# One core of a transformer block with gated attention and a mixture of experts: one norm chain for both norms, the x rows ahead of Wv and Wo, W2 split on GpSimd, the router bias inside the router weights

## The chip, the cores and the metric

One NeuronCore of one Trainium2 chip runs the whole program. The metric is the device time of one execution in microseconds (us). A core has TensorE (PE), VectorE (DVE), ScalarE (ACT), GpSimd (POOL) and SyncE (SP), which here only issues DMAs. Every engine takes its own instructions strictly in order and waits on semaphores.

## The reference

128 batches of 64 rows of 128 features are normed, attend to a context with 16 heads and a mask that is added, and are added back; the sum is normed again and goes through eight experts, of which each row uses its best two.

```python
def xattn(q, k, v, attn_mask, Wq, Wk, Wv, Wo, num_heads):
    qh, kh, vh = proj_heads(q, Wq), proj_heads(k, Wk), proj_heads(v, Wv)
    scores = einsum('bhqd,bhkd->bhqk', qh, kh) + attn_mask
    probs = softmax(scores, axis=-1)
    ctx = einsum('bhqk,bhkd->bhqd', probs, vh)
    return einsum('bse,de->bsd', ctx.transpose(0, 2, 1, 3).reshape(b, s, -1), Wo)

def ffn(x, Wg, bg, W1, b1, W2, b2):
    logits = xf @ Wg + bg
    w, idx = top_k(softmax(logits), 2)
    w = w / sum(w)
    comb = sum(one_hot(idx, 8) * w[..., None], axis=1)
    h = relu(einsum('nd,edh->enh', xf, W1) + b1[:, None, :])
    y = einsum('enh,ehd->end', h, W2) + b2[:, None, :]
    return einsum('end,ne->nd', y, comb)

x = x + tanh(g_xattn[0]) * xattn(layernorm(x), ctx, ctx, mask, Wq, Wk, Wv, Wo, 16)
x = x + tanh(g_ffn[0]) * ffn(layernorm(x), Wg, bg, W1, b1, W2, b2)
```

## The kernel before

**Numbers in two halves.** Every float32 operand of a product is held as a float16 high part and a float16 low part (names end in H and L), and each product is three matmuls (`three_passes`, lines 49 to 52): high by high, low by high, high by low. So each result in a PSUM bank is read twice: ACT writes the high part from the bank, and DVE, or POOL by way of a float32 copy in SBUF, writes the low part as the difference. Weights are scaled by WS = 32 before they are split.

**Groups and steps.** A group is eight batches (512 rows); there are 16 groups. Each engine has one loop over steps s, eight to a group (`for s in range(FIRST, LAST)`), and inside a step it works on several stages at once: the queries of the next group (two heads a step), values and scores of batch s, the softmax of batch s-1, the transposed probabilities of batch s-2, probabilities times values of batch s-3, and expert s-16 of the group two before. Step i of a group has the extra work: in step 4 the statistics of the second norm and both norm chains on POOL, in step 5 the normed rows on ACT, in step 6 the transposes of x, the context and x2 on PE, in step 0 the router logits, in steps 1 to 4 the ranks, the two gate weights and the bias b2. The order in each engine's loop is written by hand. For the first group the loop begins at s = -8.

**PSUM.** Two banks belong to the scores. The other six go round in turn (`take_bank`, `evicted`): a stage that takes a bank waits until the readers of whatever held it six turns earlier are done. PE therefore waits for DVE, ACT and POOL both through operands and through banks.

**The opening.** Ahead of the loop PE multiplies Wq by Wk (line 392, four banks), transposes Wv and Wo (line 403), then the normed rows of the first group (line 282). ACT norms these rows (line 527) before it takes the first weight bank. DVE takes the low halves of all weights, those of Wg and b2 included (line 661), and only then the low half of the transposed rows (line 686), which the first query waits for. SP loads Wq, Wk, x, Wv, Wo, Wg, b2 in this order, then the rest. W1 gets the bias b1 added and is split by ACT and DVE in steps 6 and 10, W2 in steps 11 and 12 (`SPLIT_W`).

**The norm chain** (`ln_scale_shift`, POOL, lines 896 to 905) is four instructions for each norm and group: variance plus EPS, power -1/2, minus the mean, shift. In step 4 it runs twice in a row, for the first norm of group g+2 and the second of group g-1. Behind it on POOL stands the low part of the hidden values (line 920), which the expert's second product waits for.

**The logits** (DVE, line 851): the bank is scaled and the bias `bgrow` added into SBUF tensor `logit`; `above` and `same` (lines 859, 860) compare each with each, then maximum and difference to it (861, 863). All four read `logit` in SBUF. The bank is free after line 851.

## Time and profile before

| | |
|---|---|
| median of 3 runs | 1015.77 us (1014.31 to 1018.8) |
| the profiled execution | 1016.24 us, of which the span of its instructions is 1014.5 us |
| PE busy | 976.2 us |
| DVE, ACT, POOL busy | 858.9, 865.7, 786.5 us |
| PE clock granted, mean over the span | 0.998 of full |
| DMA | 56.92 MB, mean 56 GB/s |

Busy time is the union of an engine's instructions; what PE is not busy it waited, and the profile names the releaser. A wait for several semaphores is put down to the one that came last.

### The profile page before, as it was taken

Reading aid. Unit: us, or ns where it says so; the run is one execution under the profiler, and the core shown is the slowest. Engines: PE = TensorE matmul, PEld = TensorE weight load, DVE = VectorE, ACT = ScalarE, POOL = GpSimd, SP = SyncE. Lnnn points to the kernel's source line nnn. Section 1 sums busy time; section 2 is a strip of 40 time slices with the busy share of each in tenths; the row PEclk is TensorE's granted clock in tenths of the full one; section 3 lists DMA queues with packets and bytes.
Section 4 is the critical chain, followed back from the end, with each engine's and each line's share of the span. In section 5 each row is a group of like instructions: output and inputs, shape, how many; then the busy total and the mean of one; then the engine's idle time right before and its main releaser. Section 6 shows DMA issues by size and latency. Waiting matters only on the chain.

```text
span 1014.5 us, 36079 instructions
## 1 busy us (share of the span) xinstructions
PE 976.2 (96%) x13762; PEld 733.5 (72%) x13762; DVE 858.9 (85%) x1754; ACT 865.7 (85%) x1740; POOL 786.5 (78%) x799
## 2 busy tenths in 40 slices
PE   6899799999999999999999999999999999999897
PEld 4467577777777777777777777777777777778775
DVE  3899998988979889798888979898897988879687
ACT  3799889898998989989898998989899898989743
POOL 4155578788888878888887888878888887889955
PEclk9999999999999999999999999999999999999999
DMA  9334332232232233322323233233223322323100
GB/s 209 65 62 76 58 60 43 55 64 54 47 61 57 49 57 53 65 45 49 59 54 60 49 65 54 43 57 62 53 51 58 59 38 44 54 34 61 26 13 22
DMA packets 319978, 56.92 MB, mean 56 GB/s; under 512 B 288920, under 2 KB 319680, under 8 KB 319808
## 3 DMA queue, kind: packets, MB, share of 16 engines
q1 hardware_dynamic: 319808, 54.61, 29.8%
q8 instruction: 112, 1.84, 0.8%
q14 instruction: 58, 0.48, 0.2%
HBM read 16.82 MB, written 4.19 MB: 21 GB/s over the span
## 4 chain that ended last, share of the span: by engine, by line
PE 67%; POOL 13%; DVE 7%; ACT 6%; issue 6%; DMA 1%; POOLq 0%; SPq 0%; DVEq 0%; ACTq 0%
PE bank L50 20%; PE bank L52 20%; PE bank L51 20%; PE bank L327 4%; POOL hidL L920 4%; POOL rstd L901 3%; POOL ptL L970 2%; PE bank L282 2%; DVE above L859 2%; POOL prob L976 1%; DVE y_scaled L747 1%; ACT pt L596 1%; ACT bank L539 1%; ACT vH L576 1%; ACT qH L488 1%
## 5 line engine op out<-in xcount | busy, mean ns | idle before, releaser
L920 POOL TENSOR_TENSOR hidL<-hid,hidH 128x512 f16<-128x512 f32 x228 | 261.1, 1162 | 0.0
L970 POOL TENSOR_TENSOR ptL<-pt,ptH 128x512 f16<-128x512 f32 x128 | 148.5, 1160 | 126.9 <-ACT pt L596 126.8
L681 DVE TENSOR_TENSOR qL<-bank,qH 128x512 f16<-128x512 f32 x248 | 169.4, 686 | 42.5 <-ACT qH L488 37.1
L488 ACT ACTIVATE qH<-bank 128x512 f16<-128x512 f32 x256 | 153.7, 603 | 46.0 <-PE bank L52 44.1
L50 PE MATMUL bank<-w2H,hidH 128*128 128x128 f16 x1024 | 178.1, 219 | 6.1 <-POOL hidL L920 5.7
L965 POOL TENSOR_TENSOR x<-x,y_scaled 128x512 f32<-128x512 f32 x128 | 163.4, 1277 | 21.1 <-DVE x L765 15.7
L52 PE MATMUL bank<-w2H,hidL 128*128 128x128 f16 x1024 | 178.1, 219 | 0.0
L51 PE MATMUL bank<-w2L,hidH 128*128 128x128 f16 x1024 | 178.1, 219 | 0.0
L514 ACT ACTIVATE hidH<-bank 128x512 f16<-128x512 f32 x256 | 166.5, 652 | 12.7 <-PE bank L52 12.0
L505 ACT ACTIVATE hid<-bank 128x512 f32<-128x512 f32 x228 | 146.8, 644 | 0.0
L976 POOL TENSOR_TENSOR prob<-prob,row_inv 128x512 f32<-128x512 f32 x128 | 133.7, 1045 | 2.7 <-DVE row_inv L793 1.9
L747 DVE SCALAR_TENSOR_TENSOR y_scaled<-bank,out_scale,weight 128x512 f32<-128x512 f32 x128 | 95.1, 743 | 42.5 <-PE bank L52 39.9
L50 PEld LDWEIGHTS bank<-w2H,hidH 128*128 128x128 f16 x1024 | 100.1, 98 | 17.5 <-issue 9.9
L51 PEld LDWEIGHTS bank<-w2L,hidH 128*128 128x128 f16 x1024 | 100.1, 98 | 7.6
L50 PE MATMUL bank<-xtH,aH 128*128 128x512 f16 x256 | 98.2, 383 | 6.4 <-DVE qL L681 3.1
L50 PEld LDWEIGHTS bank<-ctH,qH 128*128 128x128 f16 x1024 | 92.3, 98 | 15.2 <-issue 0.2
L50 PE MATMUL bank<-ptH,vdH 128*128 128x64 f16 x1024 | 103.0, 193 | 0.2 <-issue 0.2
L52 PE MATMUL bank<-ctH,qL 128*128 128x64 f16 x1024 | 103.1, 193 | 0.0
L52 PE MATMUL bank<-ptH,vdL 128*128 128x64 f16 x1024 | 103.1, 193 | 0.0
L51 PE MATMUL bank<-ctL,qH 128*128 128x64 f16 x1024 | 103.1, 193 | 0.0
L51 PE MATMUL bank<-ptL,vdH 128*128 128x64 f16 x1024 | 103.1, 193 | 0.0
L50 PE MATMUL bank<-ctH,qH 128*128 128x64 f16 x1024 | 103.0, 193 | 0.0
(145 smaller groups left out, 3444.8 us busy)
## 6 DMA issues: line engine op xcount, KB each, us to landing
vdH<-vH SPq DMA_DIRECT2D x256, 64.0 KB, 2.3
vdL<-vL SPq DMA_DIRECT2D x256, 64.0 KB, 2.3
x_raw<-in_x SPq DMA_DIRECT2D x16, 256.0 KB, 3.1
ctx_raw<-in_ctx SPq DMA_DIRECT2D x16, 256.0 KB, 3.2
mask_raw<-in_fside_Bx1xSxS SPq DMA_DIRECT2D x32, 128.0 KB, 2.9
out_x<-x SPq DMA_DIRECT2D x16, 256.0 KB, 2.6
qH<-in_L_xattn_Wq SPq DMA_DIRECT2D x2, 256.0 KB, 4.9
qH<-in_L_xattn_Wk SPq DMA_DIRECT2D x2, 256.0 KB, 5.6
```

Source lines behind the costliest of these rows:

```text
L50: e.matmul(dst, lhs[0], rhs[0], start=start, stop=False, skip_group_check=True)
L51: e.matmul(dst, lhs[0], rhs[1], start=False, stop=False, skip_group_check=True)
L52: return e.matmul(dst, lhs[1], rhs[0], start=False, stop=stop, skip_group_check=True)
L488: act.activation(qH[:, g % 2, 2 * j + g2, :, h2, :], bk("Q", g, h)[:, :].rearrange("p (b q) -> p b q", b=GB), ACT.Copy).then_inc(s_q_high, 1)
L505: act.activation(hid[:, k % NR, :], bk("hid", g, e, c)[:, :], ACT.Relu).then_inc(s_relu[c], 1)
L514: act.activation(hidH[:, m % 2, c, :], bk("hid", g, e, c)[:, :], ACT.Relu).then_inc(s_hid_high[c], 1)
L681: dve.tensor_tensor(qL[at], bk("Q", g, h)[:, :].rearrange("p (b q) -> p b q", b=GB), qH[at], ALU.subtract).then_inc(s_q_low[h % 2], 1)
L747: dve.scalar_tensor_tensor(y_scaled[:, m % 2], bk("y", yg, yi)[:, :].rearrange("p (t d) -> p t d", t=GT), out_scale[:, 1:2], weight3[:, :, ...
L920: pool.tensor_tensor(hidL[:, m % 2, c, :], hid[:, k % NR, :], hidH[:, m % 2, c, :], ALU.subtract).then_inc(s_hid_low[c], 1)
L965: pool.tensor_tensor(acc, acc, y_scaled[:, m % 2], ALU.add).then_inc(s_y_add, 1)
L970: pool.tensor_tensor(ptL[:, b % 2, :], pt[:, b % 2, :], ptH[:, b % 2, :], ALU.subtract).then_inc(s_pt_low, 1)
L976: pool.tensor_tensor(p, p, row_inv[:, b % NPB, :].unsqueeze(2).to_broadcast([P, JG, S]), ALU.mult).then_inc(s_normal, 1)
```

## The change

Five edits, in the order of the program.

1. **Loads and opening order.** SP loads x after the first halves of Wq and Wk, ahead of their second halves. PE transposes the normed rows ahead of Wv and Wo; ACT takes two weight banks before it norms the rows, and its high half of the transposed rows, like DVE's low half, moves ahead of Wv and Wo.
2. **Wg and b2** have their own SBUF tensors, and their halves are taken in step 3 and not in the opening.
3. **The router bias**: bg/8 minus the first row of Wg is added to all rows of Wg in step 0 (a small DVE instruction more); the logit bank then holds logits with bias, scaled by 32. DVE copies the bank to `logit`, and the comparisons read one operand from the copy and one from the bank, the maximum and the difference the bank alone; the bank is free only after these. The exponent takes the scale.
4. **W2** is split by POOL in steps -4 and -2, three instructions of 128x1024 for each half, and no longer by ACT and DVE in steps 11 and 12.
5. **The norm chain** (`norm_scale_shift`) runs once per group for both norms, on 128x8 where there were two of 128x4, in the order variance, minus the mean, power, shift.

```diff
+NORM_LAG = 3
-SPLIT_W = (6, 10, 11, 12)
+SPLIT_W1 = (6, 10)
+SPLIT_W2 = (-4, -2)
...
+        wg_in = sb("wg_in", [P, E])
+        b2_in = sb("b2_in", [STACK, D])
...
+            if kind == "logit":
+                return [(s_gt, at[0] + 1), (s_eq, at[0] + 1), (s_gshift, at[0] + 1)]
...
 @block.tensor
             pe.wait_ge(s_ident, 1)
+            transposes("xT", 0, xhat, (s_ln[0]["rows"], 1), s_xT)
             for k, (what, raw) in enumerate((("Wv", wv_raw), ("Wo", wo_raw))):
...
-            transposes("xT", 0, xhat, (s_ln[0]["rows"], 1), s_xT)
...
 @block.scalar
-                    act.wait_ge(s_wdve, H // 4 + 6)
+                    act.wait_ge(s_wpe, H // 4 + 4)
...
             def ln_rows(w, g, src, dst, freed):
-                act.wait_ge(s_ln[w]["shift"], g + 1)
+                act.wait_ge(s_norm_shift, g + 1 + (NORM_LAG if w else 0))
...
-            ln_rows(0, 0, x_raw[:, 0], xhat[:, :, :], None)
             for n in range(H // 4):
+                if n == 2:
+                    ln_rows(0, 0, x_raw[:, 0], xhat[:, :, :], None)
...
+            transposed_high("xT", 0, xtH[:, 0, :], s_xT, None, s_xT_high)
...
+                if s == 3:
+                    act.wait_ge(s_wg_lifted, 1)
+                    act.activation(wgH[:, :], wg_raw, ACT.Copy, scale=WS).then_inc(s_wact, 1)
+                    act.wait_ge(s_load["b2"], 16 * 3)
+                    act.activation(b2_halves[:, :], b2_raw, ACT.Copy, scale=WS).then_inc(s_wact, 1)
...
-                if s in SPLIT_W[2:]:
-                    n = SPLIT_W.index(s) - 2
-                    act.wait_ge(s_load["W2" + "ab"[n]], 16)
-                    act.activation(flat_w2[0][:, n * 1024:(n + 1) * 1024], w2_raw[n], ACT.Copy, scale=WS).then_inc(s_wact, 1)
...
 @block.vector
+            transposed_low("xT", 0, xtL[:, 0, :], xtH[:, 0, :], s_xT_high, s_xT_low)
...
-            weights_low(H // 4 + 4, wgL[:, :], wg_raw, wgH[:, :])
-            weights_low(H // 4 + 5, b2_halves[QUAD:QUAD + E, :], b2_raw[QUAD:QUAD + E], b2_halves[QUAD:QUAD + E, :])
-            transposed_low("xT", 0, xtL[:, 0, :], xtH[:, 0, :], s_xT_high, s_xT_low)
...
+                    dve.tensor_tensor(wg_raw, wg_raw, bgrow[:, :], ALU.add).then_inc(s_wg_lifted, 1)
+                if s == 3:
+                    weights_low(H // 4 + 4, wgL[:, :], wg_raw, wgH[:, :])
+                    weights_low(H // 4 + 5, b2_halves[QUAD:QUAD + E, :], b2_raw[QUAD:QUAD + E], b2_halves[QUAD:QUAD + E, :])
...
-                    l, m, e_ = logit[:, g % 2], logit_max[:, g % 2], expo[:, g % 2]
+                    l = bk("logit", g - 2)[:, 0:GT * E].rearrange("p (t e) -> p t e", t=GT)
+                    m, e_ = logit_max[:, g % 2], expo[:, g % 2]
...
-                    dve.scalar_tensor_tensor(l, bk("logit", g - 2)[:, 0:GT * E].rearrange("p (t e) -> p t e", t=GT),
-                                             1.0 / WS, bgrow[:, :].unsqueeze(1).to_broadcast([P, GT, E]), ALU.mult,
-                                             ALU.add).then_inc(s_logit_in, 1)
-                    lj = l.unsqueeze(2).to_broadcast([P, GT, E, E])
+                    dve.tensor_copy(logit[:, g % 2], l).then_inc(s_logit_in, 1)
+                    lj = logit[:, g % 2].unsqueeze(2).to_broadcast([P, GT, E, E])
                     li = l.unsqueeze(3).to_broadcast([P, GT, E, E])
...
 @block.gpsimd
+            def norm_scale_shift(k):
+                both = slice(0 if k < GROUPS else 1, 2 if k >= NORM_LAG else 1)
+                for w, n in ((0, k), (1, k - NORM_LAG)):
+                    if within(n, GROUPS):
+                        pool.wait_ge(s_ln[w]["aggr"], n + 1)
+                        if n:
+                            pool.wait_ge(s_ln[w]["rows"], n)
+                pool.tensor_scalar(rstd[:, both], meanvar[:, both, :, 1], EPS, None, ALU.add).then_inc(s_norm_var, 1)
+                pool.tensor_scalar(minus_mean[:, both], meanvar[:, both, :, 0], -1.0, None, ALU.mult).then_inc(s_norm_minus, 1)
+                pool.wait_ge(s_norm_var, k + 1)
+                pool.tensor_tensor(rstd[:, both], rstd[:, both], minus_half[:, both], ALU.pow).then_inc(s_norm_rstd, 1)
+                pool.wait_ge(s_norm_rstd, k + 1)
+                pool.wait_ge(s_norm_minus, k + 1)
+                pool.tensor_tensor(shift[:, both], minus_mean[:, both], rstd[:, both], ALU.mult).then_inc(s_norm_shift, 1)
...
+                if s in SPLIT_W2:
+                    n = SPLIT_W2.index(s)
+                    half = slice(n * 1024, (n + 1) * 1024)
+                    pool.wait_ge(s_load["W2" + "ab"[n]], 16)
+                    pool.tensor_scalar(flat_w2[0][:, half], w2_raw[n], WS, None, ALU.mult).then_inc(s_w2_high, 1)
+                    pool.tensor_scalar(w2_raw[n], w2_raw[n], WS, None, ALU.mult).then_inc(s_w2_scaled, 1)
+                    pool.wait_ge(s_w2_high, n + 1)
+                    pool.wait_ge(s_w2_scaled, n + 1)
+                    pool.tensor_tensor(flat_w2[1][:, half], w2_raw[n], flat_w2[0][:, half], ALU.subtract).then_inc(s_w2, 1)
...
-                if within(g + 2, GROUPS) and i == 4 - sooner:
-                    ln_scale_shift(0, g + 2)
-                if within(g - 1, GROUPS) and i == 4:
-                    ln_scale_shift(1, g - 1)
+                if within(g + 2, GROUPS + NORM_LAG) and i == 4 - sooner:
+                    norm_scale_shift(g + 2)
```

How the instructions move on two engines. On DVE in the opening, before the change (aL, wvL and woL are low halves of weights, xtL that of the first rows, qL of the queries):

```order
L661 SCALAR_TENSOR_TENSOR aL<-bank,aH 128x512 [waits weights_high] x4
L705 SCALAR_TENSOR_TENSOR wvL<-bank,wvH 128x256 [waits weights_high]
L705 SCALAR_TENSOR_TENSOR wvL<-bank,wvH 128x256
L705 SCALAR_TENSOR_TENSOR wvL<-bank,wvH 128x256 [waits weights_high]
L705 SCALAR_TENSOR_TENSOR wvL<-bank,wvH 128x256
L661 SCALAR_TENSOR_TENSOR woL<-bank,woH 128x512 [waits weights_high] x2
L661 SCALAR_TENSOR_TENSOR wgL<-qL,wgH 128x8 [waits weights_high]
L661 SCALAR_TENSOR_TENSOR b_halves<-qL,b_halves 8x128 [waits weights_high]
L686 TENSOR_TENSOR xtL<-bank,xtH 128x512 [waits xT_high]
L681 TENSOR_TENSOR qL<-bank,qH 128x8x64 [waits q_high] x4
```

The same place with the change:

```order
L662 SCALAR_TENSOR_TENSOR aL<-bank,aH 128x512 [waits weights_high] x4
L687 TENSOR_TENSOR xtL<-bank,xtH 128x512 [waits xT_high]
L707 SCALAR_TENSOR_TENSOR wvL<-bank,wvH 128x256 [waits weights_high]
L707 SCALAR_TENSOR_TENSOR wvL<-bank,wvH 128x256
L707 SCALAR_TENSOR_TENSOR wvL<-bank,wvH 128x256 [waits weights_high]
L707 SCALAR_TENSOR_TENSOR wvL<-bank,wvH 128x256
L662 SCALAR_TENSOR_TENSOR woL<-bank,woH 128x512 [waits weights_high] x2
L682 TENSOR_TENSOR qL<-bank,qH 128x8x64 [waits q_high] x4
```

xtL stood behind twelve instructions on weights and now stands behind the four aL alone.

On POOL, from the last fill of the opening to the first low half of queries of group 1, before:

```order
L946 MEMSET vdL 128x4096
L899 TENSOR_SCALAR rstd<-meanvar 128x4 [waits ln0_aggr,minus_half]
L901 TENSOR_TENSOR rstd<-rstd,minus_half 128x4 [waits ln0_var]
L902 TENSOR_SCALAR minus_mean<-meanvar 128x4
L905 TENSOR_TENSOR shift<-minus_mean,rstd 128x4 [waits ln0_minus,rstd0]
L899 TENSOR_SCALAR rstd<-meanvar 128x4 [waits ln0_rows,ln0_aggr]
L901 TENSOR_TENSOR rstd<-rstd,minus_half 128x4 [waits ln0_var]
L902 TENSOR_SCALAR minus_mean<-meanvar 128x4
L905 TENSOR_TENSOR shift<-minus_mean,rstd 128x4 [waits ln0_minus,rstd0]
L913 TENSOR_TENSOR qL<-hid,qH 128x8x64 [waits q_out1,q_high]
```

With the change, from the second of these chains on:

```order
L900 TENSOR_SCALAR rstd<-meanvar 128x4 [waits ln0_rows,ln0_aggr]
L901 TENSOR_SCALAR minus_mean<-meanvar 128x4
L903 TENSOR_TENSOR rstd<-rstd,minus_half 128x4 [waits norm_var]
L906 TENSOR_TENSOR shift<-minus_mean,rstd 128x4 [waits norm_minus,norm_rstd]
L958 TENSOR_SCALAR w2H<-y_scaled 128x1024 [waits loaded_W2a]
L959 TENSOR_SCALAR y_scaled<-y_scaled 128x1024
L962 TENSOR_TENSOR w2L<-y_scaled,w2H 128x1024 [waits w2_scaled,w2_high]
L958 TENSOR_SCALAR w2H<-x 128x1024 [waits loaded_W2b]
L959 TENSOR_SCALAR x<-x 128x1024
L962 TENSOR_TENSOR w2L<-x,w2H 128x1024 [waits w2_scaled,w2_high]
L914 TENSOR_TENSOR qL<-hid,qH 128x8x64 [waits q_out1,q_high]
```

Six instructions of 128x1024 now stand between that chain and the queries' low half (w2_raw lies in the tensors y_scaled and x2 until they are needed), and minus_mean has moved ahead of the power.

## Rows read from the trace of the kernel before

**Rows 1.** Page, part 1: busy us of each engine (share of the span), instructions
```profile
PE 976.2 (96%) x13762; PEld 733.5 (72%) x13762; DVE 858.9 (85%) x1754; ACT 865.7 (85%) x1740; POOL 786.5 (78%) x799
```

**Rows 2.** Waits of PE, 160 to 900 us: releaser, us, times, longest
```profile
PE bank L50 <- POOL hidL L920: 5.0, 12, 0.4
PE bank L50 <- DVE y_scaled L747: 2.1, 12, 0.2
```

**Rows 3.** Waits of PE, 900 to 1000 us
```profile
PE bank L50 <- DVE y_scaled L747: 0.8, 2, 0.5
PE bank L50 <- POOL hidL L920: 0.7, 1, 0.7
```

**Rows 4.** Waits of PE, 95 to 125 us
```profile
PE bank L327 <- POOL prob L976: 4.6, 3, 2.9
```

**Rows 5.** Timeline of the opening: start us, us, instruction, count, [idle before, releaser]
```profile
6.52 7.16 PE L392 MATMUL bank<-qH 64*128 64x128 f32 x32 [4.12 <-DMA qH<-in_L_xattn_Wk]
...
7.27 3.50 POOL L946 MEMSET vdL<- 128x4096 f16 x1
...
11.66 0.23 POOL L899 TENSOR_SCALAR rstd<-meanvar 128x4 f32<-128x4 f32 x1 [0.89 <-DVE meanvar L674]
...
13.72 1.65 ACT L527 ACTIVATE xhat<-x_raw,shift,rstd 128x128 f32<-128x128 f32 x4 [11.65 <-POOL shift L905]
...
16.13 2.22 SPq L1029 DMA_DIRECT2D x<-in_L_ffn_W  x1
...
16.73 1.94 PE L403 MATMUL bank<-ident,qL 128*128 128x128 f32 x8 [1.15 <-DVE aL L661]
...
18.46 1.06 PE L282 MATMUL bank<-ident,xhat 128*128 128x128 f32 x4
...
22.11 0.58 PE L50 MATMUL bank<-xtH,aH 128*128 128x512 f16 x1 [2.58 <-DVE b_halves L661]
```

**Rows 6.** Timeline of PE and of POOL after the opening, 32 to 47 us
```profile
35.01 0.44 PE L50 MATMUL bank<-xtH,aH 128*128 128x512 f16 x1 [2.50 <-DVE qL L681]
...
46.64 1.16 POOL L913 TENSOR_TENSOR qL<-hid,qH 128x512 f16<-128x512 f32 x1 [14.66 <-ACT hid L496]
```

**Rows 7.** Timeline of DVE, steps 11 and 12: the low halves of W2
```profile
98.92 1.90 DVE L661 SCALAR_TENSOR_TENSOR w2L<-y_scaled,w2H 128x1024 f16<-128x1024 f32 x1
...
106.08 1.22 DVE L661 SCALAR_TENSOR_TENSOR w2L<-x,w2H 128x1024 f16<-128x1024 f32 x1
```

**Rows 8.** Timeline of POOL in step 4 of one group: two norm chains
```profile
460.76 0.23 POOL L899 TENSOR_SCALAR rstd<-meanvar 128x4 f32<-128x4 f32 x1
461.07 1.04 POOL L901 TENSOR_TENSOR rstd<-rstd,minus_half 128x4 f32<-128x4 f32 x1
...
462.87 0.23 POOL L899 TENSOR_SCALAR rstd<-meanvar 128x4 f32<-128x4 f32 x1
```

**Rows 9.** Timeline of DVE and of PE around that step
```profile
460.04 0.38 DVE L674 BATCH_NORM_AGGREGATE meanvar<-stats 128x2 f32<-128x6 f32 x4
...
466.14 0.22 PE L50 MATMUL bank<-w2H,hidH 128*128 128x128 f16 x1 [0.42 <-POOL hidL L920]
```

**Rows 10.** Timeline of DVE, POOL and PE in step 0 of a group: the logits
```profile
490.19 1.14 DVE L859 TENSOR_TENSOR above<-logit 128x256 f32<-128x256 f32 x1
491.25 0.41 DVE L860 TENSOR_TENSOR same<-logit 128x256 f32<-128x256 f32 x1
...
491.79 0.73 DVE L863 TENSOR_TENSOR expo<-logit,logit_max 128x32 f32<-128x32 f32 x1
492.44 0.74 DVE L747 SCALAR_TENSOR_TENSOR y_scaled<-bank,out_scale,weight 128x512 f32<-128x512 f32 x1
...
491.74 0.73 POOL L991 TENSOR_TENSOR same<-same,tri 128x256 f32<-128x256 f32 x1 [0.69 <-DVE same L860]
...
493.24 0.39 PE L50 MATMUL bank<-x2tH,w1H 128*128 128x512 f16 x1 [0.18 <-DVE y_scaled L747]
```

**Rows 11.** One stretch, busy us: PE, PEld, DVE, ACT, POOL, PEclk, DMA share, GB/s
```profile
36.00:42.00 6.00, 6.00 (x45) 3.17 (x44) 5.63 (x10) 5.13 (x11) 0.00 (x0) 0.78 0.00 0
```

71 lines of the change are left out of this document (26 added, 45 removed).

## The prediction

> **What bounds the kernel now.** I read the page first, then the waits of PE by stretch, then the timeline of each place that the change touches. PE is busy 976.2 of 1014.5 us [rows 1], so 38.3 us of waiting is all that an edit can win which leaves the matmuls alone, and this one does. The reader should see where that idle time lies. In each regular group PE waits 0.4 us once for the hidden values' low part on POOL and 0.2 us once for y_scaled on DVE: 5.0 + 2.1 = 7.1 us in the twelve groups from 160 to 900 us [rows 2]; two more groups bring 0.8 + 0.7 = 1.5 us [rows 3]. In steps 11 to 13, while the weights of the experts are still being split, PE waits 4.6 us for POOL's probabilities, once for 2.9 us [rows 4]. In the opening it waits 2.58 us ahead of the first query [rows 5], and 2.50 us more nine queries later [rows 6].
>
> **Opening.** Before, POOL waited 0.89 us for the statistics of x and began its chain at 11.66; ACT began the normed rows 2.06 us later, at 13.72, and only after them the first weight bank [rows 5]. With x loaded third, the statistics come before POOL has finished its fills, so that POOL begins at 11.66 - 0.89 = 10.77 (the 3.50 us fill that starts at 7.27 ends there). The chain loses the 0.24 us instruction between power and shift, which now runs beside the wait for the variance: 1.8 us. ACT starts the rows at 12.6, having taken two banks already, and is done 1.65 us later, at 14.25. PE ends Wq by Wk at 6.52 + 7.16 = 13.68, waits 0.6, transposes the rows (1.06 us), then Wv and Wo in two sets of eight at 1.94 us each: 14.3 + 1.0 + 3.9 = 19.2. DVE's low half of the rows falls under those transposes, so the first query starts at 19.2 and not 22.11: **2.9 us**. Both ends: with POOL as late as before, still the rows' transposes no longer stand behind two sets of transposes, and the low part of b2, which the first query waited for [rows 5], is gone: 1.5 us; a first query that already finds PE's clock up gives 4.2. Loading x ahead of the second halves of Wq and Wk puts these back by one load, and PE takes its second eight pairs only halfway through the 7.16 us; I cost that at nothing, at most 0.3 us.
>
> **The second chain** of POOL (the rows of group 1) is what DVE and ACT then stand behind until PE resumes at 35.01 [rows 6]. It loses the same 0.24 us: **0.25 us**.
>
> **W2 on POOL.** Six instructions of 128x1024 move to where POOL idled 14.66 us, up to 46.64 [rows 6]. No row has this shape. From below, the fill of 4096 elements in 3.50 us [rows 5] gives 0.9 us for 1024; from above, twice the 1.16 us of a two-operand 128x512 [rows 6] gives 2.3. So 5.4 to 14 us; I take 8, nearer the fill for the four with one operand. The room is 14.7 us, and both ends fit: **0**. SP issues the last W2 load by 16.13 + 2.22 = 18.35 [rows 5], ten microseconds ahead of POOL's turn. Rule and row here pull apart only in the size: the Trainium skill (GPSIMD Engine Reference, section 4.1, Engine selection) says elementwise work belongs on VectorE and is about twice as slow on GpSimd. By that rule alone the six cost twice what DVE paid, and the move would be wrong if POOL had a queue behind it; here the queue is empty.
>
> What the move takes away: DVE's 1.90 + 1.22 = 3.1 us of W2 low parts [rows 7], and ACT's two high halves, in the stretch where DVE has no idle time and PE waits 4.6 us for what DVE feeds to POOL [rows 4]. I take 3.0 for these. In step 12 the two chains become one, which frees POOL earlier for the probabilities, but ACT's first four rows now wait for the statistics of both norms; I put the balance at 0.7. Together **3.7 us**; ends 2.0 (PE catches another releaser) and 5.9 (4.6 and the smaller waits beside it, all gone).
>
> **What is put into step 0 and step 3.** A small addition in step 0 and the halves of Wg and b2 in step 3 are three small instructions more on DVE and two on ACT, of some 0.2 us each going by the 0.23 of POOL's [rows 8], where DVE is nearly full. PE is idle there only now and then, so I charge **-0.4 us**, ends 0 and -0.8.
>
> **The joined chain in the regular groups.** POOL starts the first chain at 460.76, the second at 462.87: 2.11 us for each [rows 8]. Both sets of statistics are there by 460.42 [rows 9], so the joined one need not wait. Its price turns on the power: 1.04 us on four elements a partition [rows 8], against 0.23 for the addition of the same shape ahead of it [rows 8]. If that is fixed, the joined chain takes 1.9 us; if it is per element, eight cost 2.0 and the chain 2.9. Either way the hidden values' low part comes 1.3 to 2.3 us earlier, and PE's wait for it is 0.42 [rows 9]. It goes entirely.
>
> **The logits.** DVE's `above` takes 1.14 us and `same`, with the same operands' shape, 0.41; the difference of 32 elements takes 0.73 and ends as POOL's `same` does (491.74 + 0.73 = 492.47) [rows 10]. An instruction with two SBUF operands thus stands still while POOL works. With one operand in PSUM they do not compete: 0.41 and about 0.2, **1.2 us** earlier for y_scaled, which PE waits 0.18 for [rows 10]. That wait goes too. The Trainium skill (SBUF — State Buffer, SBUF: two separate sides) calls the pair of ports shared by VectorE and GpSimd an exclusive lock, held for a whole instruction; by that rule, the trace agrees. The bank is held about a microsecond longer, but the stage that takes it next is the one behind PE's instruction at 493.24 [rows 10], 2 us after DVE will be done with it.
>
> Regular groups and the two late ones: **7.1 + 1.5 = 8.6 us**.
>
> **Sum.** 2.9 + 0.25 + 3.7 - 0.4 + 8.6 = 15.05 us. The profiled execution took 1016.24 us, 0.47 above the median of the runs: 1001.2, or 1000.7 against the median. I say 1001.0. The worst and the best ends added give 1016 - (1.5 + 0 + 2.0 - 0.8 + 7.1) = 1006.4 and 1016 - (4.2 + 0.5 + 5.9 + 8.6) = 997.
>
> **Rivals.**
> - *The regular groups give nothing back.* Once PE waits no longer for POOL or y_scaled, another wait appears at the same places; against it, PE's idle time there has two releasers only [rows 2]. Then only the gains of the opening and steps 11 to 13 remain, 6.45 us: 1009.8. It is near the bound between faster and the same.
> - *PE's clock.* After the wait of 2.50 us [rows 6] the granted clock from 36 to 42 us is 0.78 [rows 11], which is 2.6 us at the 1.2 GHz level and the rest at 2.4. If the shorter waits keep it at the upper level, half of the 2.6 falls away, and as much again at the first queries: 998.5. Against it: PE was busy for 7.16 us at a stretch in the opening, and still the query at 22.11 ran at the lower level (0.58 us [rows 5] where the same shape takes 0.39 [rows 10]). The Trainium skill (TensorE: Matmul & The Clock Gate, Part 1: The HAM clock gate) says that the clock is released by sustained activity, which the longer run of transposes ahead of the queries would now be.
> - *POOL overruns.* If its six W2 instructions cost over 2.5 us each, POOL is late for the queries' low part at 46.64 and then for the first probabilities; at 4 us each 24 us stand against a room of 14.6, the excess of 9.4 goes straight to PE, and 5.65 us of gain are left: 1010.6.
> - *Slower: compares against PSUM.* `above` and `same` read a bank with each element repeated eight times. No row has this. The slack that the change makes ahead of y_scaled is 1.0 us a group, after the 1.2 that it saves. If each comparison takes 1.7 us and not 0.41, DVE is 2.6 us later, PE waits 1.55 us in each of 15 groups, 23.3 us, while the other gains are 15.05 - 2.9 = 12.1: 1027. It outweighs them from about 1.3 us a comparison. For it: nothing. Against it: DVE reads 512 elements of a bank for y_scaled in 0.74 us [rows 10], so 256 should be about 0.4.
> - *It doesn't do what it says*: the joined chain or the moved loads could leave the order as it was; the order of instructions shows that they don't, and I give this nothing.
>
> **Chances.** Forecast 0.78; regular groups give nothing 0.09; clock 0.06; POOL overruns 0.03; slower by the comparisons 0.04. A measurement of this kernel can tell about 0.5%, 5 us, from no change: faster is below 1010.7. The forecast, the clock and most of the first rival lie there, 0.90; within 0.5% I put the rest of that rival and the overrun, 0.06; slower 0.04. The range 996 to 1008.5 takes in these ends, widened for the parts of the first rival, and the clock, and leaves out the other rivals.
>
> **What would show it.** The first query at 19 to 20 us; POOL's six W2 instructions between 29 and 43; steps 11 and 12 without W2 on DVE and PE's waits for probabilities there under 2 us; one power of 128x8 per group, and no wait of PE on hidL or y_scaled from 160 to 900 us, with groups 0.6 us shorter; `above` at 0.4 to 0.5 us. Wrong would be groups as long as before, comparisons over a microsecond, or a first query after 21 us.

## The result, and the profile after

| | before | after |
|---|---|---|
| median, us (runs) | 1015.66 (4) | 997.71, 997.37 to 998.24 (4) |
| ratio to before | 1 | 0.9823, 95% interval 0.9807 to 0.9839 |
| profiled execution, us | 1016.24 | 997.37 |
| its span, us | 1014.5 | 995.6 |

The change makes the kernel 18 us faster. I had forecast 1001.0, 15 us, with a range of 996 to 1008.5. Busy time of the engines (the page, part 1; before in [rows 1]), and then the six largest of the twelve releasers that PE waits for in the changed kernel (waits of PE: releaser, us, times, longest):

```profile
PE 970.8 (98%) x13762; PEld 734.2 (74%) x13762; DVE 837.9 (84%) x1753; ACT 863.2 (87%) x1738; POOL 786.0 (79%) x753
```

```profile
PE bank L332 <- POOL prob L986: 6.8, 9, 2.2
PE bank L397 <- DMA qH<-in_L_xattn_Wk: 4.0, 1, 4.0
PE bank L52 <- DVE qL L682: 2.3, 1, 2.3
PE bank L52 <- DVE xtL L687: 1.6, 1, 1.6
PE bank L388 <- POOL ptH L924: 1.4, 1, 1.4
PE bank L332 <- DVE hidH L829: 0.9, 1, 0.9
```

From 160 to 900 us the view of the waits lists nothing at all where it had two releasers in twelve groups [rows 2]. Idle time is down by 38.3 - 24.8 = 13.5 us, but the span by 18.9. The difference is the main lesson of this case: the idle time that the profile shows on PE is less than what a wait costs (below).

To see where the gain arises I use a mark that both kernels have once a step: the start of DVE's row maximum of step s. How much earlier it comes than before, beside what the terms of the forecast add up to:

| from | to | gain in the traces | forecast |
|---|---|---|---|
| start | step 0 (42.94, now 37.72) | 5.22 | 2.9 + 0.25 |
| step 0 | step 4 (59.19, now 56.73) | -2.76 | -0.4 |
| step 4 | step 13 (110.44, now 104.55) | 3.43 | 3.0 |
| step 13 | step 16 (127.28, now 122.52) | -1.13 | 0.7 |
| step 16 | end of the span | 14.14 | 8.6 |
| | sum | 18.9 | 15.05 |

**Opening.** The timeline answers to [rows 5] (start us, us, instruction, count, [idle before, releaser]):

```profile
12.71 1.65 ACT L531 ACTIVATE xhat<-x_raw,shift,rstd 128x128 f32<-128x128 f32 x4 [1.92 <-POOL shift L906]
...
14.51 1.09 PE L287 MATMUL bank<-ident,xhat 128*128 128x128 f32 x4 [0.73 <-ACT xhat L531]
...
15.39 3.27 PE L409 MATMUL bank<-ident,qL 128*128 128x128 f32 x16
...
18.50 0.38 PE L52 MATMUL bank<-xtH,aH 128*128 128x512 f16 x1
```

The chain of loads, norm and rows is within 0.2 us of the forecast (12.6 for the rows, 14.3 for their transposes). But the sixteen transposes of Wv and Wo take 3.27 us and not 3.9, and the first query 0.38 and not 0.58: PE's clock is at its upper level when the queries begin. Not all of that is the clock's: in e7_spread (below), whose first query still runs at the lower level (0.63 us), the sixteen transposes take 3.62.

**W2 on POOL.** What followed in the opening is the part that I had put at nothing:

```profile
26.73 2.79 POOL L958 TENSOR_SCALAR w2H<-y_scaled 128x1024 f16<-128x1024 f32 x1
...
40.16 2.13 POOL L962 TENSOR_TENSOR w2L<-x,w2H 128x1024 f16<-128x1024 f32 x1
42.24 1.16 POOL L914 TENSOR_TENSOR qL<-hid,qH 128x512 f16<-128x512 f32 x1
43.35 1.05 POOL L986 TENSOR_TENSOR prob<-prob,row_inv 128x512 f32<-128x512 f32 x1
...
44.55 0.63 PE L332 MATMUL bank<-ident,prob 128*128 128x128 f32 x4 [1.42 <-POOL prob L986]
```

The six instructions take 15.5 us (two of them are shown; the others stand between them), and POOL goes from the last one straight into its first queries, with no idle time: it is late, and PE waits 1.42 us for the first probabilities. What PE then does, in stretches of 1 us (busy time of PE, its count, granted clock, DMA share, GB/s):

```profile
45.00:46.00 1.00, 1.00 (x6) 0.74 0.06 10
46.00:47.00 1.00, 1.00 (x4) 0.50 0.78 122
47.00:48.00 1.00, 1.00 (x4) 0.50 0.54 74
48.00:49.00 1.00, 1.00 (x15) 0.56 0.48 72
49.00:50.00 1.00, 1.00 (x29) 1.00 0.00 0
```

It works at the 1.2 GHz level from 45.5 to 48.9 us. Once its clock has come up, the kernel before has one such stretch, ahead of step 0 [rows 11]. The changed kernel has one here and one from 110.3 to 113.7; a third begins at 994, when PE is nearly done.

**Regular groups.** One joined chain, in the place of the two in [rows 8]:

```profile
450.61 0.25 POOL L900 TENSOR_SCALAR rstd<-meanvar 128x8 f32<-128x8 f32 x1
450.94 0.24 POOL L901 TENSOR_SCALAR minus_mean<-meanvar 128x8 f32<-128x8 f32 x1
451.15 1.67 POOL L903 TENSOR_TENSOR rstd<-rstd,minus_half 128x8 f32<-128x8 f32 x1
452.90 0.20 POOL L906 TENSOR_TENSOR shift<-minus_mean,rstd 128x8 f32<-128x8 f32 x1
453.06 1.15 POOL L921 TENSOR_TENSOR hidL<-hid,hidH 128x512 f16<-128x512 f32 x1
```

Two and a half us instead of 4.2; the power costs 1.04 us on four elements a partition and 1.67 on eight, between my two readings of it. And the logits, against [rows 10]:

```profile
479.46 0.42 DVE L857 TENSOR_TENSOR above<-logit,bank 128x256 f32<-128x256 f32 x1
479.80 0.41 DVE L858 TENSOR_TENSOR same<-logit,bank 128x256 f32<-128x256 f32 x1
...
480.35 0.19 DVE L861 TENSOR_TENSOR expo<-bank,logit_max 128x32 f32<-128x32 f32 x1
```

A group has become 0.93 us shorter, where I had said 0.6.

### The profile page after: what moved, and what is told of

It is laid out like the page before. It is cut to its first block, busy times and chain, and to the rows that moved or that the text cites. A ratio compares the mean times of both kernels' runs of the same rounds, so it can differ in the third digit from the quotient of the medians.

```text
span 995.6 us, 36034 instructions
## 1 busy us (share of the span) xinstructions
PE 970.8 (98%) x13762; PEld 734.2 (74%) x13762; DVE 837.9 (84%) x1753; ACT 863.2 (87%) x1738; POOL 786.0 (79%) x753
## 3 DMA queue, kind: packets, MB, share of 16 engines
q8 instruction: 112, 1.84, 0.8%
## 4 chain that ended last, share of the span: by engine, by line
PE 87%; POOL 6%; DVE 3%; issue 2%; ACT 1%; POOLq 0%; DVEq 0%; ACTq 0%
PE bank L52 26%; PE bank L54 26%; PE bank L53 26%; PE bank L332 6%; PE bank L287 2%; POOL hidL L921 1%; PE bank L468 1%; POOL prob L986 1%; POOL x L975 1%; POOL w2H L958 1%; POOL ptL L980 0%; DVE qL L682 0%; PE bank L477 0%; DVE otL L803 0%; POOL vdH L946 0%
## 5 line engine op out<-in xcount | busy, mean ns | idle before, releaser
L518 ACT ACTIVATE hidH<-bank 128x512 f16<-128x512 f32 x256 | 168.9, 661 | 13.2 <-PE bank L54 12.5
L509 ACT ACTIVATE hid<-bank 128x512 f32<-128x512 f32 x228 | 148.9, 653 | 0.0
L52 PEld LDWEIGHTS bank<-ctH,qH 128*128 128x128 f16 x1024 | 92.4, 98 | 15.3 <-issue 0.3
L52 PEld LDWEIGHTS bank<-ptH,vdH 128*128 128x128 f16 x1024 | 92.2, 98 | 14.3 <-issue 0.8
```

What stands on the lines that cost most here:

```text
L52: e.matmul(dst, lhs[0], rhs[0], start=start, stop=False, skip_group_check=True)
L509: act.activation(hid[:, k % NR, :], bk("hid", g, e, c)[:, :], ACT.Relu).then_inc(s_relu[c], 1)
L518: act.activation(hidH[:, m % 2, c, :], bk("hid", g, e, c)[:, :], ACT.Relu).then_inc(s_hid_high[c], 1)
```

## The experiments

The kernels ran in four sets (e1 to e4, e5 to e8, e9 and e10, e11 and e12), each with its own runs of the kernel before, whose median lay between 1015.96 and 1017.91 us. Kernels of one set are compared by their times, those of different sets by their ratios to the kernel before, or by their traces. The diffs are excerpts.

### One part alone, on the kernel before

**e1_join**, the joined chain:

```diff
-                if within(g + 2, GROUPS) and i == 4 - sooner:
-                    ln_scale_shift(0, g + 2)
-                if within(g - 1, GROUPS) and i == 4:
-                    ln_scale_shift(1, g - 1)
+                if within(g + 2, GROUPS + NORM_LAG) and i == 4 - sooner:
+                    norm_scale_shift(g + 2)
```

> Kernel before with the joined norm chain alone. Theory (the wait shown for PE, 0.42 us, is counted from the end of the last matmul, while the pitch of the matmuls is shorter, so that what is lost is 0.58 us): the joined chain ends the wait on hidL in the 12 regular groups and in two late ones, 14 x 0.58 = 8.1 us, and 0.25 us comes from the second chain in the opening; 1015.7 - 8.4 = 1007.3. A POOL instruction of 128x8 pow takes 1.67 us once a group, groups are 0.58 us shorter (59.57), and the wait on y_scaled stays at 0.18. Rival A (only what the waits show): 14 x 0.42 + 0.25 = 6.1, 1009.6, groups 0.42 shorter. Rival B (the two waits hide one behind the other, so that without the edit of the logits nothing is gained): 1015.5, groups as long as before, the wait on y_scaled grown to 0.6.

Measured 1009.89 (1008.87 to 1010.71), ratio 0.9930, 0.9913 to 0.9947. The time falls on rival A's price by chance: the groups are 0.58 us shorter, as the theory said. Most of what is missing is 0.9 us in the opening, where PE's clock comes up only at 27.7 us (at 25.0 in the kernel before), so that step 0 is 0.65 later and not 0.25 earlier, and 1.17 us between steps 13 and 14, the same as in the change (see e12_apart).

**e2_open**, the opening's order:

```diff
             pe.wait_ge(s_ident, 1)
+            transposes("xT", 0, xhat, (s_ln[0]["rows"], 1), s_xT)
...
-            transposes("xT", 0, xhat, (s_ln[0]["rows"], 1), s_xT)
```

> Kernel before with the new opening order alone (x loaded third, its transposes ahead of those of Wv and Wo). Theory (the 5.2 us won by the first row maximum of DVE are all the opening's; what is lost again by step 4 comes from W2 on POOL and from the small instructions of step 3): first row maximum at 37.9, and of the 5.0 us at least 4.5 are still there at step 4 and at the end; 1015.7 - 4.8 = 1010.9. Rival (steps 0 to 4 are bound by DVE whatever the opening does, so that the gain falls to 2.5 there): first row maximum at 37.9, the one of step 4 at 56.7, 1013.2.

Measured 1013.93 (1011.90 to 1013.99), ratio 0.9967, 0.9955 to 0.9979: 2 us, and not the 4.8 of the theory. Step 0 comes 3.48 us earlier, not 5.0, and steps 0 to 14 keep it, so that the rival is wrong too, though its 1013.2 is the nearer number. At step 15 1.63 us are lost, in a stretch at the lower clock from 112.2 to 115.6 us that the kernel before does not have (PE in stretches of 1 us):

```profile
113.00:114.00 1.00, 1.00 (x14) 0.50 0.00 0
114.00:115.00 1.00, 1.00 (x7) 0.50 0.12 20
```

**e3_w2pool**, W2 on POOL:

```diff
-SPLIT_W = (6, 10, 11, 12)
+SPLIT_W = (6, 10)
+SPLIT_W2 = (-4, -2)
```

> Kernel before with W2 split on POOL in steps -4 and -2 alone. POOL's six instructions take 15.5 us from 31.9 on, to 47.4; the queries' low part that POOL began at 46.64 before comes about 0.9 us late. Theory (off DVE and ACT in steps 11 and 12 they win 3.0, in the opening they lose 1 to 1.5 through POOL's lateness and the two-operand instructions of DVE that stand still beside them): 1015.7 - 1.7 = 1014.0, with the start of step 14 0.5 to 2 us earlier than before. Rival A (steps 11 to 13 are bound by the two separate norm chains of POOL there, and what W2 takes on DVE is hidden): no gain, only the loss, 1016.9. Rival B (the loss is larger, as all of what is lost between steps 0 and 4 is POOL's): 1015.2.

Measured 1015.75 (1013.71 to 1016.73), ratio 0.9991, 0.9980 to 1.0001: no gain that can be measured, where the theory had 1.7 us. The trace has both of its parts: 1.43 us lost from step 0 to 4, and 2.96 won from step 8 to 13.

**e11_logit**, Wg, b2 and the logits:

```diff
-                    dve.scalar_tensor_tensor(l, bk("logit", g - 2)[:, 0:GT * E].rearrange("p (t e) -> p t e", t=GT),
-                                             1.0 / WS, bgrow[:, :].unsqueeze(1).to_broadcast([P, GT, E]), ALU.mult,
-                                             ALU.add).then_inc(s_logit_in, 1)
-                    lj = l.unsqueeze(2).to_broadcast([P, GT, E, E])
+                    dve.tensor_copy(logit[:, g % 2], l).then_inc(s_logit_in, 1)
+                    lj = logit[:, g % 2].unsqueeze(2).to_broadcast([P, GT, E, E])
```

> Kernel before with the edits of Wg, b2 and the logits alone (bias inside the weights, their halves in step 3, comparisons with one operand in the bank); the two norm chains, the opening and W2 as before. Theory (the two waits of a group are independent, each lost time adds): above falls to 0.42, the wait on y_scaled goes (0.35 us lost in each of 14 groups, 1.4 in the first one), the wait on hidL stays at 0.42, groups of 59.80; the opening wins 1.7 (no low part of b2 ahead of the first query) and steps 3 and 4 lose up to 1.9 again: 1015.9 - 6.2 + 0.2 = 1009.9. Together with the joined chain alone (6.1) and the opening alone (2.0) this makes 14.1 of the 18. Rival (the parts hide each other, the y_scaled wait is only moved to hidL of the next expert): groups of 60.15, 1014 to 1015.

Measured 1010.87 (1010.02 to 1011.37), ratio 0.9928, 0.9916 to 0.9941; the groups are 59.80 us, as the theory said.

The four reductions are 0.70, 0.33, 0.09 and 0.72%, together 1.84%, where the whole change gives 1.77%. The medians of the sets give less, 6.1 + 2.0 + 0.2 + 7.0 = 15.3 of 18 us, and so do the spans of the profiled executions, 5.5 + 2.3 + 1.2 + 5.4 = 14.4 of 18.9. The gap does not arise in the regular groups: at step 32 the four together are 1.7 us ahead and the change 7.0. A good part of it is PE's clock, which comes up 1.0 to 2.7 us later in e1_join, e3_w2pool and e11_logit than in the kernel before, and costs e2_open 1.63 us at step 15. All the sums say which parts carry the change: the chain and the logits.

The mark of each step shows where each gains (us earlier than in the kernel before; negative is later):

| | step 0 | 4 | 13 | 14 | 16 | 17 | 32 | 112 |
|---|---|---|---|---|---|---|---|---|
| the change | 5.22 | 2.46 | 5.89 | 4.73 | 4.76 | 6.29 | 7.03 | 16.29 |
| e1_join | -0.65 | -0.64 | -0.63 | -1.80 | -1.79 | -1.80 | -0.62 | 5.17 |
| e2_open | 3.48 | 3.49 | 3.50 | 3.52 | 1.90 | 1.90 | 1.96 | 2.20 |
| e3_w2pool | -0.87 | -2.30 | 0.71 | 0.73 | 0.73 | 0.73 | 0.81 | 1.12 |
| e11_logit | -0.26 | -1.60 | -1.14 | -1.13 | -1.13 | 0.15 | -0.41 | 3.13 |

From step 32 to step 112 are ten groups. Their length follows from the marks: before (848.22 - 246.68) / 10 = 60.15 us, e1_join 59.58, e11_logit 59.80, the change 59.23. The joined chain takes 0.58 from each group, the logits 0.35, and the sum of 0.93 is what the change takes: two waits that add, and neither hides the other. In e1_join PE still waits for y_scaled, in e11_logit still for hidL, as in [rows 2] (waits of PE, 160 to 900 us, of the one and of the other):

```profile
PE bank L51 <- DVE y_scaled L748: 2.1, 12, 0.2
```

```profile
PE bank L50 <- POOL hidL L925: 5.0, 12, 0.4
```

**Why 0.58 and not 0.42.** The timeline of PE in the kernel before, around the wait of [rows 9]:

```profile
465.45 0.22 PE L51 MATMUL bank<-woL,otH 128*128 128x128 f16 x1
465.50 0.22 PE L52 MATMUL bank<-woH,otL 128*128 128x128 f16 x1
```

These matmuls of 128x128 start 0.056 us apart (465.45 and 465.50 are rounded), and each is shown with 0.22 us from start to end. The idle time of 0.42 is counted from the end of the last, 465.72, up to 466.14. But without the wait the next would have started at 465.50 + 0.056, so what is lost is 0.58. At y_scaled four transposes stand ahead, shown with 0.64 us, behind which the next instruction can start after 0.47 (in the changed kernel, 108.92 to 109.39): 493.24 - 492.42 - 0.47 = 0.35, where the profile has 0.18 [rows 10]. Both agree with the lengths of the groups to a hundredth. The forecast for e1_join had the 0.58 before it ran.

### Which half of the logits' edit matters

**e4_logit_sbuf**: the changed kernel, all four readers on the SBUF copy.

```diff
                     lj = logit[:, g % 2].unsqueeze(2).to_broadcast([P, GT, E, E])
+                    l = logit[:, g % 2]
                     li = l.unsqueeze(3).to_broadcast([P, GT, E, E])
```

> Changed kernel, but above, same, the maximum and the difference read both operands from the SBUF copy; the bias stays folded into the weights. Theory (an instruction of DVE with two SBUF operands stands still while POOL works): above takes 1.0 to 1.2 us again in most groups, the difference 0.5 to 0.7, y_scaled comes about 1 us later, PE waits for it and loses 0.35 us per group: 997.7 + 15 x 0.35 = 1002.9, groups of 59.58. Rival A (it was the folding of the bias that made them short, the operands' place doesn't matter): above stays at 0.42, 997.7. Rival B (above grows, but the joined chain has made enough room ahead of y_scaled): above at 1.1 and no wait of PE, 997.9.

Measured 1003.96 (1003.39 to 1004.16): 6.3 us slower than the changed kernel (by the ratios, 0.9871 against 0.9823, 4.9; the theory had 5.2). Groups are 59.57 us. The lines of DVE by shape (min, median and longest ns, first and last start) for e4, and below them for the change:

```profile
L858 DVE TENSOR_TENSOR above<-logit x16: 426/1132/2322, 124.8 to 975.4; 128x256 f32<-128x256 f32 x16
```

```profile
L857 DVE TENSOR_TENSOR above<-logit,bank x16: 420/420/422, 124.7 to 969.5; 128x256 f32<-128x256 f32 x16
```

The same instruction on the same shape takes 0.42 us with one operand in PSUM, and up to 2.3 with both in SBUF. The folding of the bias into the weights wins nothing by itself (its groups are as long as those of e1_join, 59.58); it is what allows the operand to stay in the bank. The timeline of e4 in one group shows DVE held until POOL is done, at 482.61, and `above` ending 0.28 us behind that; in the groups before it the distance is 0.28 or 0.29 us as well:

```profile
481.45 1.16 POOL L922 TENSOR_TENSOR hidL<-hid,hidH 128x512 f16<-128x512 f32 x1
481.76 1.13 DVE L858 TENSOR_TENSOR above<-logit 128x256 f32<-128x256 f32 x1
```

So an instruction of DVE with two SBUF operands stands still until an instruction of POOL with two operands is done. The Trainium skill (SBUF — State Buffer, SBUF: two separate sides) calls it an exclusive lock, held for the whole instruction; by that rule, the trace agrees here. It does not for POOL's multiplications by a constant (e7_spread, below).

### What the opening gave back

**e5_w2back**: the changed kernel, W2 split by ACT and DVE in steps 11 and 12 again.

```diff
+                if s in (11, 12):
+                    n = s - 11
+                    act.wait_ge(s_load["W2" + "ab"[n]], 16)
+                    act.activation(flat_w2[0][:, n * 1024:(n + 1) * 1024], w2_raw[n], ACT.Copy, scale=WS).then_inc(s_wact, 1)
```

> Changed kernel with W2 split by ACT and DVE in steps 11 and 12 again, as before; all other edits kept. Theory (W2 on POOL costs in the opening what it wins in steps 11 to 13: POOL is free only at 42.3, 0.9 us late for its first queries, PE waits 1.42 us for the probabilities and then runs 3.4 us at the 1.2 GHz level): the start of step 4 is 1.5 to 2.3 us earlier than in the changed kernel and has no stretch at half the clock ahead of it, the start of step 14 is about 0.7 later, and the whole is within 1.5 us of the changed kernel: 998.5. Rival (what I forecast: the move is worth 3 us and costs nothing): 1000.7, with step 4 where it is in the changed kernel.

**e6_small**: all that Wg and b2 need, in step -5.

```diff
-                if s == 0:
+                if s == -5:
                     dve.wait_ge(s_load["bg"], 16)
...
-                if s == 3:
+                if s == -5:
                     weights_low(H // 4 + 4, wgL[:, :], wg_raw, wgH[:, :])
```

> Changed kernel with the addition to Wg and the halves of Wg and b2 in step -5, where ACT waits for the shift and DVE has no work, and nothing of them in steps 0 and 3. Theory A (of the 2.76 us lost between steps 0 and 4 the instructions put into step 3 take the larger part, since step 3 to 4 alone loses 1.85): step 4 starts 1.5 to 1.9 us earlier than in the changed kernel, 996.0. Theory B (the loss is POOL's lateness and the stretch at half the clock that follows PE's wait): step 4 starts at most 0.6 us earlier, 997.2 to 997.7. A loss of some tenths is possible if ACT's part delays its rows: step 0 would then start later.

**e7_spread**: the second half of W2 behind the probabilities of steps 5, 6 and 7.

```diff
-SPLIT_W2 = (-4, -2)
+SPLIT_W2 = ((-4, -4, -4), (5, 6, 7))
```

> Changed kernel, but POOL takes only the first half of W2 in the opening (step -4), and the three instructions of the second half behind the probabilities of steps 5, 6 and 7, where it has gaps of 2.9 to 3.3 us. Theory B (POOL's lateness): POOL is free long before its first queries, PE's wait of 1.42 us for the probabilities falls to 0.6, no stretch at half the clock stands at 45 to 49 us, step 4 starts 0.9 to 2.8 us earlier, and it stays won: 996.0. Theory A (the small instructions of step 3): step 4 at most 0.5 us earlier, 997.3. If the gaps of POOL are too small for 2.8 us instructions, PE waits for ptL or the probabilities in steps 5 to 8 and the gain is given back: 998.

**e8_rows**: ACT's rows of group 1 one step later.

```diff
-                if i == 5 - sooner and within(g + 2, GROUPS):
+                if i == (4 if s < 0 else 5) and within(g + 2, GROUPS):
                     ln_rows(0, g + 2, x_raw[:, (g + 2) % NX], xhat[:, :, :], (s_xT, g + 2))
```

> Changed kernel with ACT's rows of group 1 one step later in the opening, so that ACT does not stand for 2.33 us at the shift of POOL while banks of queries wait. Theory (PE's wait of 2.29 us at 27.5 is ACT's wait for the shift and its 1.65 us of rows, put ahead of the queries): the wait falls to about 1 us and is followed by a smaller one for the rows; step 0 starts 1 to 1.7 us earlier, 996.4. Rival (the first wait only moves to the transposes of these rows, or PE's clock falls after the new pattern of waits): step 0 where it was or later, 997.7 to 999.

| | us | ratio, 95% interval | step 0 | 3 | 4 | 7 | 14 | 32 |
|---|---|---|---|---|---|---|---|---|
| e5_w2back | 999.47 | 0.9827, 0.9809 to 0.9844 | 0.05 | 0.90 | 1.46 | 1.46 | -1.51 | -1.97 |
| e6_small | 996.76 | 0.9799, 0.9782 to 0.9816 | -0.70 | 0.19 | 1.24 | 0.77 | 0.76 | 0.18 |
| e7_spread | 997.74 | 0.9807, 0.9789 to 0.9825 | -1.12 | -0.27 | 0.29 | -0.45 | -0.43 | -0.90 |
| e8_rows | 998.37 | 0.9819, 0.9797 to 0.9840 | 1.84 | 0.04 | 0.00 | -0.01 | -0.02 | -0.18 |

(The marks are here us earlier than in the changed kernel.) No interval excludes that one of the four is as fast as the change, and e7_spread (996.0 forecast) and e8_rows (996.4) missed their theories. The traces say more:

- Without W2 on POOL step 4 comes 1.46 us earlier, and no stretch at the lower clock stands there; in steps 11 and 12, 1.46 + 1.51 = 2.97 us are lost. So my 3.0 for ACT and DVE was right, and the nothing for POOL should have been 1.5.
- The 0.70 and 1.12 us that e6_small and e7_spread have lost by step 0 are not their edits'. They have them already at PE's first long wait, at 30.50 and 30.92 us against 29.80: PE's clock comes up 0.8 and 1.7 us after their first query. From step 0 to step 4 e6_small gains 1.94 us and e7_spread 1.41.
- The 2.76 us lost there have three parts. Us from mark to mark:

| | step 0 to 3 | 3 to 4 | lower clock between |
|---|---|---|---|
| before, e9_best | 10.89 | 5.36 | no |
| the change | 11.80 | 7.21 | yes |
| e3_w2pool | 11.79 | 5.89 | yes |
| e6_small | 10.91 | 6.16 | no |
| e5_w2back, e7_spread | 10.95 | 6.65 | no |

- Up to step 3, 0.9 us are lost only where the stretch at the lower clock is. e6_small has W2 on POOL as the change has, and PE's wait for it, but not the stretch (below: timeline of PE, and PE in stretches of 1 us). From step 3 to 4, POOL's lateness costs 0.6 to 0.8 us and the small instructions 1.0 to 1.3, of which 0.2 are lost to both. Theory A and theory B are both right, each for a part, and the 1.94 of e6_small holds the 0.9 of the clock.

```profile
45.26 0.41 PE L332 MATMUL bank<-ident,prob 128*128 128x128 f32 x2 [1.43 <-POOL prob L986]
```

```profile
47.00:48.00 1.00, 1.00 (x16) 1.00 0.70 104
```

- e8_rows wins 1.84 us at step 0 and has lost them at step 3. The place is one line (timeline of PE): POOL is where it was, so PE, who comes earlier, waits longer.

```profile
44.49 0.63 PE L332 MATMUL bank<-ident,prob 128*128 128x128 f32 x4 [3.21 <-POOL prob L986]
```

- e7_spread gave back 0.7 us at step 6. Timeline of POOL and DVE in it, and of DVE in the changed kernel: the low half of W1, which has two SBUF operands, now stands beside an instruction of POOL.

```profile
69.47 2.77 POOL L934 TENSOR_SCALAR x<-x 128x1024 f32<-128x1024 f32 x1
...
69.64 1.95 DVE L662 SCALAR_TENSOR_TENSOR w1L<-hidH,w1H 128x1024 f16<-128x1024 f32 x1 [0.63 <-ACT w1H L641]
```

```profile
69.92 1.23 DVE L662 SCALAR_TENSOR_TENSOR w1L<-hidH,w1H 128x1024 f16<-128x1024 f32 x1 [0.63 <-ACT w1H L641]
```

It grows by 0.72 us and ends at 71.59, before POOL's instruction, which ends at 72.24. In e6_small the low part of b2 likewise takes 1.06 us (0.28 in the kernel before, where POOL is idle) inside a multiplication of POOL of 2.79. So beside this one-operand form DVE is held for some 0.7 to 0.8 us and not for the whole instruction; why, these runs do not show.

**e9_best** joins the three, with W2's instructions placed clear of step 6 and the rows of e8.

```diff
+SPLIT_W2 = ((-4, -4, -4), (-2, 5, 7))
...
-                if s == 3:
+                if s == -4:
                     act.wait_ge(s_wg_lifted, 1)
...
-                if i == 5 - sooner and within(g + 2, GROUPS):
+                if i == (4 if s < 0 else 5) and within(g + 2, GROUPS):
```

> Changed kernel with three moves joined: ACT's rows of group 1 one step later in the opening (won 1.84 us at step 0 and lost them to POOL's lateness by step 3); W2 on POOL spread so that POOL is free when its first queries come: the first half and one instruction of the second in the opening, the other two in steps 5 and 7, which keep clear of the split of W1 in step 6, where a 128x1024 of DVE grew from 1.23 to 1.95 us beside POOL; Wg and b2 in steps -5 and -4, ahead of ACT's rows. Theory (the three losses are separate places of one chain): step 0 earlier by 1.0 to 1.8 than in the changed kernel, step 4 by 3.5 to 4.5, most of it kept; 994.0. Rival A (steps 5 to 13 are bound by DVE, whatever comes before gives at most what the single moves gave, 1.2): 996.5. Rival B (the new pattern of waits makes PE's clock fall elsewhere, 1.7 us each): 995.5.

Measured 993.31 (993.05 to 994.42), ratio 0.9777, 0.9762 to 0.9791: faster than the change. Step 0 comes 2.09 us earlier than in the changed kernel, step 4 4.85, and 4.4 are left at step 14. All of the 2.76 us between steps 0 and 4 are back, and the 1.84 that e8_rows had won at step 0 and lost now stay: the wait for POOL that ate them is gone. The other two moves were not stopped by one another; alone they show 1.24 and 0.29 us at step 4 because their profiles had lost 0.70 and 1.12 to the clock before step 0. e9_best has no stretch at the lower clock before 990 us.

### The clock, and step 12

**e10_fill**: the changed kernel with eight matmuls more, whose result is overwritten, in the wait ahead of the second stretch at the lower clock.

```diff
                 for freed in take_bank("PT", b):
                     pe.wait_ge(*freed)
+                for _ in range(8 if b in (11,) else 0):
+                    pe.matmul(bk("PT", b)[:, :], aH[:, 0, :], wvH[:, 0, :, :].rearrange("p c d -> p (c d)"),
+                              start=True, stop=True)
```

> Changed kernel with eight matmuls of 128x512 more, whose result is overwritten, in PE's wait of 2.15 us for the probabilities of step 13; they add no work that the reference asks for. Theory (the stretch at half the clock from 110.3 to 113.8 follows from that wait, and costs 1.2 us, the loss between steps 13 and 14): the granted clock stays at the upper level there, step 14 starts 1.0 to 1.3 us earlier, 996.6. Rival A (the stretch is there, but DVE or ACT sets step 14, so that PE's slow stretch costs nothing): clock up, step 14 where it was, 997.7. Rival B (it doesn't hang on this wait): clock still at half from 110 to 114, time unchanged.

Measured 997.57 (997.40 to 997.79), as the change. The clock is 1.00 from 109 to 114 us now, where the changed kernel has it like this (PE in stretches of 1 us, e10 and the change):

```profile
110.00:111.00 1.00, 1.00 (x26) 1.00 0.00 0
111.00:112.00 1.00, 0.92 (x9) 1.00 0.09 16
112.00:113.00 1.00, 0.55 (x3) 1.00 0.45 63
```

```profile
110.00:111.00 1.00, 1.00 (x15) 0.66 0.07 16
111.00:112.00 1.00, 1.00 (x6) 0.50 0.06 10
112.00:113.00 1.00, 1.00 (x6) 0.50 0.74 111
```

But step 14 does not move, and only at step 16 are 0.4 us won: rival A. PE at full speed waits there for DVE (0.53 us for qL, 0.38 for otL), which is what sets these steps. So the stretch costs 0.4 us at most of the 1.7 that half the clock over 3.4 us would make, and my reading of the loss between steps 13 and 14 fell.

**e12_apart**: e9_best with the two chains one after the other in step 12 alone.

```diff
+                for part in ([[p] for p in norms] if k == NORM_LAG else [norms]):
```

> The kernel with the three moves joined, and in step 12 alone, where the statistics of the second norm come last, the two norm chains of POOL one after the other again (two of 128x4); joined in all other groups. Theory (the 1.16 us lost between steps 13 and 14 is ACT's wait for a shift that now needs both statistics): step 14 starts 1.0 to 1.2 us earlier than in that kernel, and it stays: 992.2. Rival (PE's wait for the probabilities grows by what POOL takes longer, 0.3 to 1.5 us, and eats it): 993.3 to 993.6.

Measured 992.73 (992.28 to 993.21), ratio 0.9751, 0.9738 to 0.9765. The mark is 0.15 us behind that of e9_best at step 13, 1.14 ahead of it at step 14, and 0.83 at step 32. That is the loss: in step 12 of the changed kernel the second norm's statistics come last (DVE's at 102.48, the first norm's at 101.33), and ACT waits 1.16 us for a shift that needs both. Timeline of POOL in e12_apart, where the first shift no longer waits for the second statistics:

```profile
99.16 0.20 POOL L912 TENSOR_TENSOR shift<-minus_mean,rstd 128x4 f32<-128x4 f32 x1
99.45 0.24 POOL L906 TENSOR_SCALAR rstd<-meanvar 128x4 f32<-128x4 f32 x1
```

PE's wait for the probabilities of step 13 stays at 2.1 us, so the rival falls. This kernel has the best ratio of all, 0.975 against 0.982 of the change; from e9_best only the trace tells it apart, as the two intervals overlap.

## Why the prediction was right, and where its terms were off

- **The opening, 2.9 us.** The mechanism and each time up to the transposes of x were right. The term was short by 2 us at step 0, mostly by the clock: seven matmuls of the first queries take 1.51 us where they took 2.89. I had given 0.06 to PE's clock being up at the first queries. In the profiled executions of the ten kernels with the new order it was up at the first query in seven, and came up 0.8 to 1.7 us later in e2_open, e6_small and e7_spread.
- **The second chain, 0.25.** PE's wait of 2.50 us [rows 6] is now 2.29.
- **W2 on POOL, 0.** This is the step that failed. My bound "from above, twice the 1.16 us of a two-operand 128x512 [rows 6] gives 2.3" was none: the four instructions with one operand and a factor take 2.76 to 2.79 us, the two with two operands 2.12 and 2.13. I had taken the one with one operand for the cheaper. The sum was 15.5 us and not 8, the room 14.7, and the rival of POOL's overrun, 0.03, came true in small: about 1.5 us, of which 0.9 are the stretch at the lower clock. The Trainium skill (GPSIMD Engine Reference, section 4.1, Engine selection) has one-input work on GpSimd at about line rate and only two-input work about twice slower than on VectorE; I had quoted the factor for all six. Here the trace has the one-input form as the dearer, 2.76 to 2.79 us against 2.12.
- **Off DVE and ACT in steps 11 and 12, 3.0.** Measured 2.97, and 2.96 in e3_w2pool.
- **The joined chain in step 12, +0.7.** Wrong in sign: -1.2. I wrote that ACT's rows now wait for both statistics, and then took a balance instead of costing it from DVE's order. e12_apart has the 1.2 back.
- **Steps 0 and 3, -0.4.** Measured -1.3 from step 0 to 4 in e11_logit, and -1.0 in e6_small without what it owes to the clock. I counted five short instructions; the low part of b2 alone took 1.09 us beside POOL, since it has two SBUF operands, and the place was one where DVE and ACT both set the pace.
- **The regular groups, 8.6.** Both mechanisms right, the size short by a third: 0.58 + 0.35 a group and not 0.42 + 0.18. The rest of the 14.1 us behind step 16 is the logits of the first router (1.3 to 1.5 us at step 17, in the change and in e11_logit) and of the last ones.
- **The slower case**, comparisons of 1.7 us against a bank, did not happen: 0.42 and 0.41.
- **The clock, as a rival at 998.5.** Its number is nearer to the measured 997.71 than mine, and half of its mechanism came true: the first queries ran at the upper level (1.4 us), and the stretch ahead of step 0 is gone. But two others took its place, from 45.5 and from 110.3 us, and the groups alone gave 9.3 us from step 32 to step 112, where the 8.6 was meant for all of them.
- **The ends.** The worst end as it is printed, from 1016, is 1006.2; 1006.4 is from 1016.24. Nothing hangs on it. The result lies 0.7 us from the best end, 997, because the terms that were too small outweighed those that were too large, and not because each came out at its best.

So the forecast came out 3.3 us above the result with errors of both signs: 2.1 + 0.4 + 5.5 too little for the opening, steps 4 to 13 and the groups, 2.4 + 1.8 too much for steps 0 to 4 and step 12, which is 3.8 us between the traces. That the total is only 3.3 us off is in part luck: the terms missed by 12 us in all.

## What to carry to other kernels

A wait's idle time counts from the end of the last matmul, while a matmul starts every 0.056 us and lasts 0.22: cost a wait by the starts (start after the wait, less the start before it and one pitch), or the forecast of many small waits is short by a third, as here. Before work is moved to an idle engine, bound it by an instruction of the same kind, and ask what that engine must do next: 0.9 us too late there went with a loss of 1.5 us. And before a move is called worthless, compare from a mark just ahead of it, with the clock's row beside it: here PE's clock had taken up to 1.1 us before the edit began, and one move's 1.84 us were eaten by a wait that another move removes.
